# A gated delta-rule recurrence on VectorE: two products and two row sums of 512 elements, or one of each with 1024

## The reference, cut to what matters

```python
q = (x @ Wq + bq).reshape(batch, seq, H, D)          # 16 heads of 16
k = ...; v = ...; k = k / (norm(k) + 1e-06); beta = sigmoid(x @ Wbeta + bbeta)
def _step(Sm, inputs):                                # Sm: batch, head, 16 (d), 16 (e)
    q_t, k_t, v_t, beta_t = inputs
    Sk = jnp.einsum('bhde,bhe->bhd', Sm, k_t)
    delta = v_t - Sk
    Sm = Sm + beta_t[..., None] * jnp.einsum('bhd,bhe->bhde', delta, k_t)
    o_t = jnp.einsum('bhde,bhe->bhd', Sm, q_t)
    return (Sm, o_t)
_, outputs = jax.lax.scan(_step, S0, (q, k, v, beta)) # 512 steps, one after the other
```

## Time and profile before

| what | value |
|---|---|
| timed runs | 5365.44, 5374.25, 5375.87 us |
| span of the profiled execution | 5350.8 us |
| VectorE busy | 4041.4 us, 76% of the span |
| TensorE matmuls busy | 3356.5 us, 63% |
| ScalarE busy | 1954.0 us, 37% |
| GpSimd busy | 1658.9 us, 31% |
| first and last instruction of the recurrence's product with the key | 150.0 and 2628.7 us |

### The profile page before, as it was taken

The page is one execution under the profiler, slowest core; times in us unless marked ns, Lnnn a source line. Parts: engine busy times, 40 slices in busy tenths (PEclk is TensorE's granted clock), DMA queues, the critical chain, the costliest instruction groups (busy, mean ns, idle before and its releaser), DMA issues.

```text
span 5350.8 us, 70373 instructions
## 1 busy us (share of the span) xinstructions
PE 3356.5 (63%) x20044; PEld 2319.2 (43%) x20044; DVE 4041.4 (76%) x10447; ACT 1954.0 (37%) x4826; POOL 1658.9 (31%) x2672
## 2 busy tenths in 40 slices
PE   6413056174562745326465887888689878887785
PEld 3201033163431634225353655564366655665574
DVE  1999988999889998999835665677566657775543
ACT  3101022032221322113123655565356545565453
POOL 1000001501515014230436113423721164326555
PEclk8555567597675976569677999998799989999998
DMA  1300000264212642136453333431233333443566
GB/s 51 131 34 7 3 12 32 80 187 127 86 38 91 188 121 85 38 123 190 119 154 128 94 97 107 141 117 40 89 91 99 96 121 119 137 122 120 187 211 194
DMA packets 409530, 562.91 MB, mean 105 GB/s; under 512 B 55617, under 2 KB 299457, under 8 KB 408513
## 3 DMA queue, kind: packets, MB, share of 16 engines
q1 hardware_dynamic: 360000, 424.14, 26.1%
q0 software_dynamic: 49152, 134.28, 7.6%
HBM read 349.80 MB, written 208.40 MB: 104 GB/s over the span
## 4 chain that ended last, share of the span: by engine, by line
DVE 47%; PE 32%; issue 8%; POOL 5%; ACT 4%; DMA 3%; SPq 0%; DVEq 0%; ACTq 0%; POOLq 0%
DVE rec L1188 5%; DVE skb L1193 5%; DVE rec L1190 5%; DVE rec L1204 4%; DVE rec L1201 4%; PE psum L1107 4%; DVE psum L1306 4%; DVE region L1196 4%; PE psum L955 3%; POOL xbuck L1766 2%; PE psum L1124 2%; PE psum L1007 2%; PE psum L899 2%; PE psum L993 2%; PE psum L995 1%
## 5 line engine op out<-in xcount | busy, mean ns | idle before, releaser
L1775 POOL DMA_INDIRECT yg<-ybuck,words x512 | 541.0, 1057 | 893.7 <-DMA ybuck<-yrow 415.6
L1107 PE MATMUL psum<-xgT,w 128*128 128x128 f32 x4400 | 628.6, 289 | 27.7 <-DMA w<-in_w13T 8.6
L1107 PEld LDWEIGHTS psum<-xgT,w 128*128 128x128 f32 x4400 | 575.9, 203 | 60.9 <-issue 52.4
L1766 POOL DMA_INDIRECT xbuck<-srow,words x512 | 528.6, 1032 | 152.6 <-issue 126.3
L887 PE MATMUL psum<-w_ident,xn 128*128 128x128 f32 x512 | 104.3, 340 | 728.6 <-ACT xn L1490 720.5
L1124 PE MATMUL psum<-w_w2T,hid 128*128 x1100 | 376.9, 426 | 289.5 <-DVE hid L1457 217.2
L1306 DVE CUSTOM_DVE_ANT_0 psum<-psum,xo 128x128 f32<-128x128 f32 (+3 forms) x1024 | 473.3, 517 | 105.9 <-PE psum L976 104.5
L1654 ACT ACTIVATE xgT<-psum 128x256 f32<-128x256 f32 x662 | 253.0, 382 | 672.6 <-PE psum L1089 671.0
L1619 ACT ACTIVATE region<-psum 128x512 f32<-128x512 f32 (+3 forms) x1024 | 401.0, 440 | 228.2 <-PE psum L995 219.3
L1747 POOL TENSOR_SCALAR_AFFINE_SELECT region<-region 128x128 f32<-128x128 f32 x1024 | 287.6, 298 | 527.7 <-ACT region L1619 518.9
L1134 DVE SCALAR_TENSOR_TENSOR sil<-sil,psum 128x128 f32<-128x128 f32 (+1 forms) x418 | 123.6, 296 | 388.5 <-ACT sil L1669 362.6
(11 more groups left out here) (207 smaller groups left out, 7796.7 us busy)
## 6 DMA issues: line engine op xcount, KB each, us to landing
w<-in_w13T SPq DMA_DIRECT2D x550, 256.0 KB, 3.0
xg<-xbuck SPq DMA_DIRECT2D x662, 128.0 KB
ybuck<-yrow SPq DMA_DIRECT2D x662, 128.0 KB
xbuck<-x SPq DMA_DIRECT2D x40, 512.0 KB, 5.5
x_scratch<-res SPq DMA_DIRECT2D x64, 256.0 KB, 2.1
acc<-x_scratch SPq DMA_DIRECT2D x128, 128.0 KB
xbuck<-srow,words POOLq DMA_INDIRECT x512
yg<-ybuck,words POOLq DMA_INDIRECT x512
```

The lines of the kernel that those rows point to most:

```text
L1107: o = e.matmul(psum[:, mi, half], w13[I % 3][:, k, half], xgT[I % 2][:, k, :], start=(k == 0), stop=(k == 1), skip_group_check=True)
L1766: e.indirect_dma_start(xbuck[g % 2], bass.IndirectOffsetOnAxis(ap=posu[g % 2][:, J - ROWS0[g], k:k + 1], axis=0), srow[J % 2], None).then_ ...
L1775: e.indirect_dma_start(yg[y % 5], None, ybuck[g % 2][0:TILES_OF[g] * 128, :], bass.IndirectOffsetOnAxis(ap=posu[g % 2][:, j, k:k + 1], axi ...
```

## The change

The state's order in a partition becomes d, group, e (before: group, d, e), and the tiles `kq` and `vo` are laid out by time first. At each time, `kq` holds 32 numbers of the query and then 32 of the key. So the last query and this key stand at one fixed distance of 96 numbers in memory, and one instruction multiplies the state, read twice, with both (1024 elements, line 1204 of the new kernel). One row sum over those 1024 elements (line 1207) gives 64 sums: the output of the step before and the product with the key. They are written over the last step's query and key, in `kq`. Step 0 of a block keeps the form with 512 elements (lines 1198 and 1200), since it has no query part. The outputs are later turned from `kq` and not from `vo`. The values in `vo` are now written with a stride of two elements, because the group is the innermost index.

```diff
-    kq, vo = part(0, [2, 128, 32]), part(8192, [2, 128, 16])
+    outputs = region[:, 0:8192].rearrange("p (t s d g) -> p t s d g", s=2, d=16, g=2)[:, :, 0, :, :]
+    kq, vo = part(0, [128, 2, 2, 16]), part(8192, [128, 16, 2])
-    S, tk, tq = (rec[:, i, :].rearrange("p (g d e) -> p g d e", g=2, d=16) for i in range(3))
+    S = rec[:, 0, :].rearrange("p (d g e) -> p d g e", g=2, d=16)
+    both = rec[:, 1:3, :].rearrange("p s (d n) -> p s d n", d=16)
+    tk = rec[:, 1, :].rearrange("p (d g e) -> p d g e", g=2, d=16)
     def scan_at(q, t):
-        return 1 + 896 * q + (7 * t - 2 if t else 0)
+        return 1 + 642 * q + 5 * t
+    def query_and_key(t):
+        return region[:, 64 * t - 64:64 * t + 128].rearrange("p (s n) -> p s n", s=2)[:, :, 0:32]
+    def output_and_product(t):
+        return region[:, 64 * t - 64:64 * t]
+    def loaded_to(g, slot, e0):
+        return kq[:, :, 1 - slot, g, e0:e0 + 4] if slot < 2 else vo[:, :, e0:e0 + 4, g]
...
-                    o = e.transpose(psum[:, mi, j * 128:(j + 1) * 128], vo[:, i // 4, :, 4 * (i % 4) + j], ident[:, :])
+                    o = e.transpose(psum[:, mi, j * 128:(j + 1) * 128], outputs[:, :, 4 * (i % 4) + j, i // 4], ident[:, :])
...
-                    if slot == 2:
-                        dv.wait_ge(s["ult"], 8 * q)
-                    e.tensor_copy(dst, psum[:, mi, :].rearrange("p (e t) -> p t e", e=4)).then_inc(s["ldd"], 1)
+                    dv.wait_ge(s["ult"], 8 * q)
+                    e.tensor_copy(loaded_to(g, slot, e0), psum[:, mi, :].rearrange("p (e t) -> p t e", e=4)).then_inc(s["ldd"], 1)
...
-                    dv.wait_ge(s["scan"], c)
-                    e.tensor_tensor(tk[:, :, :, :], S[:, :, :, :], ktt, ALU.mult).then_inc(s["scan"], 1)
-                    if t:
-                        e.tensor_tensor(tq[:, :, :, :], S[:, :, :, :], bc(kq[:, :, t - 1, 16:32], 2, 16),
-                                        ALU.mult).then_inc(s["scan"], 1)
-                    dv.wait_ge(s["scan"], c + 1)
-                    e.tensor_reduce(skb[:, :, :], tk[:, :, :, :], AX.X, ALU.add).then_inc(s["scan"], 1)
-                    if t:
-                        dv.wait_ge(s["scan"], c + 2)
-                        e.tensor_reduce(vo[:, :, t - 1, :], tq[:, :, :, :], AX.X, ALU.add).then_inc(s["scan"], 1)
-                    dv.wait_ge(s["scan"], c + 2 + lag // 2)
-                    e.tensor_tensor(ub[:, :, :], vo[:, :, t, :], skb[:, :, :], ALU.subtract).then_inc(s["scan"], 1)
...
+                    else:
+                        dv.wait_ge(s["scan"], c)
+                        e.tensor_tensor(both, bc(rec[:, 0, :].rearrange("p (d n) -> p d n", d=16), 1, 2),
+                                        bc(query_and_key(t), 2, 16), ALU.mult).then_inc(s["scan"], 1)
+                        dv.wait_ge(s["scan"], c + 1)
+                        e.tensor_reduce(output_and_product(t), rec[:, 1:3, :].rearrange("p s (n e) -> p (s n) e", e=16),
+                                        AX.X, ALU.add).then_inc(s["scan"], 1)
+                        got = region[:, 64 * t - 32:64 * t].rearrange("p (d g) -> p d g", g=2)
+                    dv.wait_ge(s["scan"], c + 2)
+                    e.tensor_tensor(ub[:, :, :], vo[:, t, :, :], got, ALU.subtract).then_inc(s["scan"], 1)
```

More of the change, by code:

```diff
@@ L752, in build @@
     rec = sb("rec", [128, 3, 512])
-    skb, ub = sb("skb", [128, 2, 16]), sb("ub", [128, 2, 16])
+    skb, ub = sb("skb", [128, 16, 2]), sb("ub", [128, 16, 2])
     scale2 = [sb(f"scale{g}", [128, 2, 8, 16]) for g in range(2)]
@@ L863, in scan_at @@
     def scan_at(q, t):
-        return 1 + 896 * q + (7 * t - 2 if t else 0)
+        return 1 + 642 * q + 5 * t
     def scan_end(q):
-        return 1 + 896 * (q + 1)
+        return 1 + 642 * (q + 1)
+    def query_and_key(t):
[4 more added lines that the diff above has]
+        return kq[:, :, 1 - slot, g, e0:e0 + 4] if slot < 2 else vo[:, :, e0:e0 + 4, g]
     def rows_before(g, slot):
@@ L1180, in vector @@
                 c = scan_at(q, t)
-                lag = 2 if t else 0
-                ktt = bc(kq[:, :, t, 0:16], 2, 16)
                 if third == 0:
@@ new lines, in vector @@
+                        dv.wait_ge(s["scan"], c + 1)
+                        e.tensor_reduce(skb[:, :, :], tk, AX.X, ALU.add).then_inc(s["scan"], 1)
+                        got = skb[:, :, :]
+                    else:
+                        dv.wait_ge(s["scan"], c)
+                        e.tensor_tensor(both, bc(rec[:, 0, :].rearrange("p (d n) -> p d n", d=16), 1, 2),
+                                        bc(query_and_key(t), 2, 16), ALU.mult).then_inc(s["scan"], 1)
+                        dv.wait_ge(s["scan"], c + 1)
+                        e.tensor_reduce(output_and_product(t), rec[:, 1:3, :].rearrange("p s (n e) -> p (s n) e", e=16),
+                                        AX.X, ALU.add).then_inc(s["scan"], 1)
+                        got = region[:, 64 * t - 32:64 * t].rearrange("p (d g) -> p d g", g=2)
@@ L1205, in vector @@
+                    e.tensor_tensor(tk, bc(ub[:, :, :], 3, 16), bc(kq[:, t, 1, :, :], 1, 16),
+                                    ALU.mult).then_inc(s["scan"], 1)
+                else:
+                    dv.wait_ge(s["scan"], c + 4)
+                    e.tensor_tensor(S, S, tk, ALU.add).then_inc(s["scan"], 1)
             elif name == "step_out":
@@ L1207, in vector @@
                 dv.wait_ge(s["scan"], scan_end(q) - 2)
-                e.tensor_tensor(tq[:, :, :, :], S[:, :, :, :], bc(kq[:, :, 127, 16:32], 2, 16),
-                                ALU.mult).then_inc(s["scan"], 1)
+                e.tensor_tensor(tk, S, bc(kq[:, 127, 0, :, :], 1, 16), ALU.mult).then_inc(s["scan"], 1)
                 dv.wait_ge(s["scan"], scan_end(q) - 1)
-                e.tensor_reduce(vo[:, :, 127, :], tq[:, :, :, :], AX.X, ALU.add).then_inc(s["scan"], 1)
+                e.tensor_reduce(outputs[:, 127, :, :], tk, AX.X, ALU.add).then_inc(s["scan"], 1)
             elif name == "u_turn":
@@ L1532, in scalar @@
                     g, slot, e0 = i // 12, i % 12 // 4, 4 * (i % 4)
-                    dst = kq[:, g, :, slot * 16 + e0:slot * 16 + e0 + 4] if slot < 2 else vo[:, g, :, e0:e0 + 4]
                     ac.wait_ge(s["ldt"], 24 * q + i + 1)
                     ac.wait_ge(s["set"], 3)
[L1536 to L1539, removed]
+                    ac.wait_ge(s["scan"], scan_at(q, 0))
+                    ac.wait_ge(s["ult"], 8 * q)
+                    e.activation(loaded_to(g, slot, e0), psum[:, mi, :].rearrange("p (e t) -> p t e", e=4), ACT.Copy).then_inc(s["lda"], 1)
             elif name == "u_turn":
```

7 lines of the change are left out of this document (2 added, 5 removed).

## The result

The changed kernel takes 5426.09 us (median of 4 runs, 5414.15 to 5440.69), the kernel before 5369.84 us (median of 4, 5359.13 to 5375.87): a ratio of 1.0102, 95% interval 1.0084 to 1.0121. It is slower, by 56 us; 52 us were forecast.

What follows compares the result with a forecast made beforehand. VectorE was taken to bound the kernel, nearly always setting the time in the recurrence. Terms +56 - 6 + 2 = +52 us on 5374.25 us gave 5426 us, 1% slower, range 5395 to 5458 us.

Steps and rivals of the forecast that it cites:

- The bound: VectorE nearly always sets the time in the recurrence, 150 to about 2634 us; its change moves the end about as much.
- The merged pair, +56 us: Recurrence step: two products and two row sums, 2.40 us, become 2.50 us; 0.11 us a step over 508 steps.
- The wait behind 1024 elements: Behind each large instruction, the next start was taken to come 0.03 to 0.04 us past the record's end.
- The rival of a hidden wait: Recurrence step: the longer instruction hides the wait, gaining 76 us on VectorE, 5304 us in all; chance 4%.
- Full records as price: Recurrence step: every instruction costs its full record, waited for or not; -0.30 us a step, -152 us, 5222 us; chance 2%.
- Slack behind the borders, -6 us: First third of each later block: 108 steps grow by 12 us, half vanishing in VectorE's idle gaps; ends 0 and -12.
- Loading and turning, +2 us: Block loads: strided value copies cost 0.5 us a block, ends 0 and 16 us; TensorE's output turns 0, upper end 19.
- Sum: Whole kernel: +56 - 6 + 2 = +52 us, giving 5426 us, 1% slower.
- The first term: Recurrence: the merged products and row sums add 0.11 us a step over 508 steps, +56 us on VectorE.
- the copies' term: Block loads: value copies written with every second element cost 0.5 us a block, +2 us for four.
- What would show it: New trace: starts about 1.26 and 1.25 us apart, step 4.17 to 4.19 us, last step ending at about 2680 us.
- the small term: Loading copies out of PSUM: +2 us for strided values; wrong if those copies stay near 0.69 us.

Runs made afterwards that it cites:

- second profile of the changed kernel: Nothing changed against the changed kernel, run and profiled again on another chip: 1.0107 to the kernel before, median 5421.68 us.
- two instructions added: Changed kernel plus two unneeded 16-element sums a step, behind the large product and behind its row sum: 1.0098 to the kernel before, median 5417.00 us.
- neighbour waits: Kernel before, same seven instructions a step reordered so each row sum directly follows its product; nothing merged or resized: 1.0203 to the kernel before.
- sum merged: Changed kernel with two products of 512 elements instead of one of 1024, keeping the one row sum of 1024: 1.0159 to the kernel before.
- bare places filled: Kernel before, query's row sum cut in pieces, put behind difference, second product or addition where no other VectorE work stood: 0.9915, median 5324.77 us.

## Why the prediction was right

- **The bound.** Right. The loss lies in the recurrence: in the second profile of the changed kernel its end is 54.3 us later, and what follows takes 2716.8 us, within the scatter of that stretch (2714 to 2726 us). One reading was loose: VectorE's tenths behind slice 20 run from 3 to 7, not from 5 to 7; that stretch lies behind the recurrence and no term rests on it.
- **The merged pair, +56 us.** The mechanism held and the size was a little low: 0.12 us a step and not 0.11. Block 1 grew by 15.8 us over 127 steps, 0.124 each; for 508 steps that is 63 us. The part mis-sized is the row sum: I took 0.72 + 0.52 from a record of 678 ns that had no bare wait behind it; with one, a sum of 512 records 686 ns, and the large sum took 1.25 to 1.26 us to the next start, not 1.24.
- **The wait behind 1024 elements.** The end I chose is what stands: 0.03 to 0.04 us behind the record, as behind 32 and 512. The rival of a hidden wait is out, by the timeline and by "two instructions added", which find the slot empty.
- **Full records as price (the Trainium skill's rule, as the prediction reads it).** Out, by "neighbour waits" and "two instructions added".
- **Slack behind the borders, -6 us.** The size is not decided, and the place fits. Blocks 2 to 4 grew by 50.9 and 37.7 us in two profiles; 381 steps at 0.124 are 47 us. Cut at the addition of step 36, the growth behind it is 33.4 and 35.1 us, where 273 steps at 0.124 are 34: nothing vanishes there. In front of it, it is 17.5 and 2.6 us, where 108 steps are 13. So what differs between these two profiles lies in the stretches that the prediction named, and it is larger than the term. With double the growth ("neighbour waits") 22 of 27 us are missing in front of the cut and 11 of 68 behind it.
- **Loading and turning, +2 us.** The term is nil. Copies with a stride of two take 692 ns. Line 1152 was the nearest row but has a longer stride, and of the two distances tried, 2 and 32 numbers, only the longer one costs. From a block's last row sum to the next block's start, the three borders together grew by 1 us, no more than one differs from another. The turns at 64 numbers apart are as fast as at 16.
- **Sum.** 63, less what slack took, and 0 for the borders, against 56 measured (1.0102 with 1.0084 to 1.0121 is 45 to 65 us). The first term was 7 us low and the copies' term 2 us high. That the total came within 4 us of the forecast needs some 7 us of slack, which fits the 6 taken but lies inside the scatter: that the total came so close is partly luck.
- **What would show it.** Of the test rows, the starts (1.25 to 1.26 us apart, for 1.26 and 1.25), the step at 4.18 us and copies near 0.69 us as the case against the small term came out as written. VectorE's busy time grew by about half as much as the span: by 7.4 us where the first block's stretch grew by 16. That the last step ends at about 2680 us: 2704 in the longer of two profiles, 2689 in the other.

**What stays open:** why less of a large change arrives in blocks 2 to 4 than 381 steps ask for ("neighbour waits", 61 of 95 us; "sum merged", 59 of 73) and, in its one profile, little of a gain ("bare places filled", 8 of 39 us, though its timed gain of 46 us says that this profile is no typical one: it is the slowest of its six runs). No run was made to part slack from the scatter between executions. Nor does any run part the wait for the semaphore from the dependence on the result: every bare wait here has both, so the 0.12 us may belong to either.

## What to carry to other kernels

Read distances between starts, not lengths of records: where they are shorter than the record, the next instruction is hiding something, and a merge takes that away. Two independent chains on one engine are worth more when they alternate than when they are fused, as long as the fixed price of an instruction (0.06 us here) is below the price of a bare wait (0.12 us). Before merging, count which instructions will wait for their direct neighbour afterwards; and where such waits are bare, cut independent work in pieces and put it there, but only there: 942 pieces in bare places made this kernel 0.85% faster, and 582 more in the others gave back most of it.

## What the runs showed of the hardware

- An instruction of VectorE behind one it doesn't depend on starts 0.60 us after a start of 512 float32 elements and 0.19 us after one of 128: about 1.04 ns an element and 0.06 us fixed. Behind one it waits for, 0.72 to 0.73 us and 1.26 us for 512 and 1024: 0.19 us fixed.
- A small instruction of 16 elements fits in that difference at no cost (1.0098 with two of them in each step, 1.0107 without).
- VectorE's copy from PSUM of 512 elements takes 0.69 us with four neighbours at a time, and with every second number, and 1.03 us when every element lands 128 bytes from the last.
